# Sums of absolute weights moved to ScalarE, one norm spread over later units, one norm deferred, in a four-layer Perceiver kernel

## The reference, cut to what matters

```
x = x + L0_xattn(layernorm(x), ctx, ctx, mask)      # 16 heads over 4096 keys
x = x + L0_attn(...); x = x + L0_ffn(layernorm(x), w1, conv_w, conv_b, w2)
...                                                 # layer 1 and 2
x = x + L2_ffn(layernorm(x), W_r, W_k, W_v, mu_r, mu_k)   # sigmoid(r) * v
x = x + L3_xattn(layernorm(x), ctx, ctx, Wq, Wk, Wv, Wp, focusing_factor)
x = x + L3_attn(...); x = x + L3_ffn(...)
```

```
def weight_quant(w):
    scale = 1.0 / jnp.clip(jnp.mean(jnp.abs(w)), 1e-05)
    return jnp.clip(jnp.round(w * scale), -1, 1) / scale
```

## Time and profile before

| | us |
|---|---|
| three timed runs | 2000.08, 2008.40, 2007.03 |
| their median | 2007.03 |
| the profiled execution | 2001.91 |
| its span | 2000.6 |
| mean granted clock of PE in it | 0.989 |

### The profile page before, as it was taken

The page is one execution under the profiler, slowest core; times in us unless marked ns, Lnnn a source line. Parts: engine busy times, 40 slices in busy tenths (PEclk is TensorE's granted clock), DMA queues, the critical chain, the costliest instruction groups (busy, mean ns, idle before and its releaser), DMA issues.

```text
span 2000.6 us, 38492 instructions
## 1 busy us (share of the span) xinstructions
PE 1894.7 (95%) x14304; PEld 1204.0 (60%) x14329; DVE 1354.4 (68%) x3178; ACT 1248.9 (62%) x2811; POOL 706.3 (35%) x899
## 2 busy tenths in 40 slices
PE   7999999989999899999999999999999899899999
PEld 4555665545465645566555556879657688565656
DVE  3677668765486677766879577774356998578382
ACT  3687778867363458777888673367265786265251
POOL 2123331173460211333110155676042566355151
PEclk9999999987999999999999999999999999999999
DMA  9677668753011497766876113164102342200110
GB/s 214 145 147 150 120 120 164 127 92 106 1 43 53 77 149 148 152 118 122 164 128 93 37 52 98 49 204 123 48 22 77 93 120 61 90 1 9 43 57 11
DMA packets 114362, 191.58 MB, mean 96 GB/s; under 512 B 17224, under 2 KB 67201, under 8 KB 107649
## 3 DMA queue, kind: packets, MB, share of 16 engines
q1 hardware_dynamic: 113184, 188.11, 42.9%
q10 hardware_dynamic: 992, 1.02, 0.2%
HBM read 135.20 MB, written 2.69 MB: 69 GB/s over the span
## 4 chain that ended last, share of the span: by engine, by line
PE 66%; DVE 21%; ACT 7%; issue 2%; POOL 2%; DMA 1%; SPq 0%; POOLq 0%; ACTq 0%; DVEq 0%
DVE WK L900 10%; PE PS L837 8%; PE PS L708 8%; PE PS L738 6%; PE PS L381 5%; PE PS L389 4%; PE PS L696 4%; ACT WK L586 3%; PE PS L2499 2%; PE PS L539 2%; PE PS L2441 2%; PE PS L491 2%; PE PS L518 2%; PE PS L754 2%; PE PS L1369 1%
## 5 line engine op out<-in xcount | busy, mean ns | idle before, releaser
L900 DVE TENSOR_REDUCE WK<-PS 128x1 f32<-128x1024 f32 x512 | 621.1, 1223 | 218.4 <-PE PS L708 170.3
L1008 ACT ACTIVATE WK<-PS 128x512 f32<-128x512 f32 x840 | 464.9, 601 | 45.0 <-PE PS L708 30.8
L708 PEld LDWEIGHTS PS<-QSR,KSR 51*128 51x128 f32 x2048 | 253.3, 189 | 242.0 <-ACT WK L1008 92.0
L708 PE MATMUL PS<-QSR,KSR 51*128 51x256 f32 x2048 | 381.4, 309 | 8.9 <-DVE WK L900 0.9
L696 PE MATMUL PS<-KSR,QSR 51*128 51x512 f32 x1024 | 371.6, 452 | 3.6 <-DMA KSR<-scratch_mask 2.8
L837 PE MATMUL PS<-WK 128*32 128x256 f32 x2528 | 223.4, 400 | 0.5 <-ACT WK L992 0.5
L614 POOL TENSOR_SCALAR WK<-WK 128x256 f32<-128x256 f32 (+1 forms) x320 | 150.9, 472 | 164.3 <-ACT WK L586 62.9
L1023 POOL TENSOR_TENSOR WK<-WK 128x512 fp32r<-128x512 f32 x62 | 79.2, 1278 | 350.9 <-ACT WK L969 177.0
L696 PEld LDWEIGHTS PS<-KSR,QSR 51*128 51x128 f32 x1024 | 187.2, 187 | 13.2 <-DVE WK L900 6.5
L586 ACT ACTIVATE WK<-PS,WK 128x256 f32<-128x256 f32 (+1 forms) x320 | 140.4, 450 | 62.3 <-DVE WK L558 42.0
L1126 POOL TENSOR_SCALAR nbw<-WK 128x4 fp32r<-128x4 f32 x64 | 12.6, 197 | 314.2 <-DVE WK L906 313.3
(11 more groups left out here) (388 smaller groups left out, 3897.9 us busy)
## 6 DMA issues: line engine op xcount, KB each, us to landing
KSR<-WK SPq DMA_DIRECT2D x381, 128.0 KB
WB<-in_ctxT SPq DMA_DIRECT2D x78, 512.0 KB, 5.1
WK<-in_ctxT SPq DMA_DIRECT2D x40, 512.0 KB, 4.1
WK<-in_ctx SPq DMA_DIRECT2D x32, 512.0 KB, 3.9
WA<-in_ctxT SPq DMA_DIRECT2D x26, 512.0 KB, 5.1
QSR<-scratch_q SPq DMA_DIRECT2D x48, 128.0 KB, 4.4
WB<-in_L3f_qkv SPq DMA_DIRECT2D x2, 1536.0 KB, 6.3
WB<-in_L3f_w SPq DMA_DIRECT2D x2, 1536.0 KB, 10.2
```

Of the source, the lines that this page charges most:

```text
L708: return pe.e.matmul(tile["S", L, s, i][:, j * 256:j * 256 + 256], KS[s % 4][HALF[i % 2], kt * 128:(kt + 1) * 128], QS[HALF[i % 2], g % 2, ...
L900: dv.e.tensor_reduce(mt[:, n:n + 1], tile["R", L, s, n].rearrange("p a b -> p (a b)"), AX, ALU.max).then_inc(*dv.at("R", L, s, n))
L1008: ac.e.activation(PR[n % NPR], tile["S", L, s, i], ACT.Exp).then_inc(*ac.at("E", L, s, i))
```

## The change

Five edits:

- **A.** POOL's `magnitude` and `total` go. ACT instead takes |w| of 1024 columns with one instruction that also adds them up (`accum_out`), four times: behind the exponentials (26,5), (26,13), (27,5) and (27,9) of layer 0's cross attention. PE waits for the last of them at `M(28)` and adds two columns for each matrix, so four products stand where two stood.
- **B.** In layer 2's tail DVE only multiplies; the sum into X goes to POOL, one instruction for all four blocks, at the end of its u = 3. Mean and variance of the four blocks are taken by DVE at u = 4 to 7. ACT makes 1/sqrt by a logarithm and an exponential at u = 7, DVE the shift at u = 8, POOL the four normalised blocks at u = 8, PE the transposes at u = 9, with the banks of `ring3`.
- **C.** The queries are projected at u = 10, not 5. `again` becomes `{2: 7, 3: 9, 15: 9, 17: 9}`, and the transposes have no `filled`.
- **D.** `l2f` ends for DVE after the multiplications, so `l3x_sp` starts there.
- **E.** Of the four norms at `M(9)`, `M(17)`, `M(25)`, `M(33)` the first moves behind the row maximum `R(10,4)`, in both layers.

```diff
-        def turn_pe(tag, src, of, *by, filled=(0, 0, 0, 0)):
+        def turn_pe(tag, src, of, *by, filled=(0, 0, 0, 0), ring=None):
...
-                b = take(banks, (tag, f), (by[f], tag, f))
+                b = take(banks if ring is None else ring, (tag, f), (by[f], tag, f))
...
+        ABS = ((26, 5), (26, 13), (27, 5), (27, 9))
...
                     if L == 0 and s == 28:
+                        pe.wait_ge(ac, "wabs", 3)
                         for i in range(2):
-                            pe.wait_ge(po, "wabs", i)
                             pe.e.matmul(b.ap[:, 1, 384 + i:385 + i], onesf[:, :], wst[:, 4 * i:4 * i + 1], start=True,
+                                        stop=False)
+                            pe.e.matmul(b.ap[:, 1, 384 + i:385 + i], onesf[:, :], wst[:, 4 * i + 3:4 * i + 4], start=False,
                                         stop=True).then_inc(*pe.at("wsum", i))
...
+                    if s == 10 and n == 4:
+                        normalise(*late)
...
                     if s >= 2 and hh == 7:
...
+                        if s == 9:
+                            late = (g, bb)
                         else:
+                            normalise(g, bb)
...
                     ac.e.activation(PR[n % NPR], tile["S", L, s, i], ACT.Exp).then_inc(*ac.at("E", L, s, i))
+                    if L == 0 and (s, i) in ABS:
+                        j = ABS.index((s, i))
+                        ac.wait_ge(pe, "F", L, 23, 7)
+                        ac.wait_ge(d_l0f)
+                        ac.wait_ge(ac)
+                        ac.e.activation(WK[:, 16384:17408], WA[:, 1024 * j:1024 * j + 1024], ACT.Abs,
+                                        accum_out=wst[:, j // 2 * 4 + j % 2 * 3:j // 2 * 4 + j % 2 * 3 + 1]).then_inc(
+                            *ac.at("wabs", j))
...
-                    if L == 0 and s == 25:
-                        magnitude(0, 0)
-                        magnitude(0, 1)
-                    if L == 0 and s == 26:
-                        total(0)
-                        magnitude(1, 0)
-                    if L == 0 and s == 27:
-                        magnitude(1, 1)
-                        total(1)
...
                 dv.e.tensor_tensor(RR[:, t, :], tile["v2f", t][:, 0:256], RR[:, t, :], ALU.mult).then_inc(*dv.at("v2f", t))
-                dv.wait_ge(dv)
-                dv.e.tensor_tensor(X[:, t, :], X[:, t, :], RR[:, t, :], ALU.add).then_inc(*dv.at())
-                if t == NT - 1:
-                    end(dv, "l2f")
-                ln_a("ln3x", X, t)
-                if t:
-                    ln_b("ln3x", X, XN, t - 1)
-            ln_b("ln3x", X, XN, NT - 1)
+            end(dv, "l2f")
...
-        unit = [*range(1, 6), 0, *range(6, NU)]
+        unit = [*range(1, 11), 0, *range(11, NU)]
...
-            again = {2: 7, 3: 26, 10: 9, 17: 9}
+            again = {2: 7, 3: 9, 15: 9, 17: 9}
...
-                if u == 3:
-                    turn_pe("h3x", XN, (dv, "ln3x"), dv, ac, filled=(10, 4, 4, 0))
+                if u == 9:
+                    turn_pe("h3x", XN, (po, "ln3x"), dv, ac, ring=ring3)
...
-                if u == 3:
+                if u == 8:
+                    dv.wait_ge(ac, "ln3x", "rs")
+                    dv.e.scalar_tensor_tensor(out=wst[:, 16:20], in0=mv[:, :, 0], scalar=-1.0, in1=rs[:, :], op0=ALU.mult,
+                                              op1=ALU.mult).then_inc(*dv.at("ln3x", "mr"))
+                if u == 9:
                     turn_dve("h3x", 0)
                 if u < NU:
                     low3_dve(u)
+                if 4 <= u < 8:
+                    dv.wait_ge(po, "x2f")
+                    ln_a("ln3x", X, u - 4)
...
-                if u == 2:
-                    ln_act("ln3x")
-                    ac.e.preload_act_table_set("natural_log_exp_and_others")
-                if u == 3:
+                if u == 7:
+                    ac.wait_ge(dv, "ln3x", "var", NT - 1)
+                    ac.e.activation(rs[:, :], mv[:, :, 1], ACT.Ln, bias=epsl[:, 0:1], scale=1.0).then_inc(*ac.at())
+                    ac.wait_ge(ac)
+                    ac.e.activation(rs[:, :], rs[:, :], ACT.Exp, scale=-0.5).then_inc(*ac.at("ln3x", "rs"))
+                if u == 9:
                     turn_act("h3x", 1)
...
+                if u == 3:
+                    po.wait_ge(dv, "v2f", NT - 1)
+                    po.e.tensor_tensor(X[:, :, :], X[:, :, :], RR, ALU.add).then_inc(*po.at("x2f"))
+                if u == 8:
+                    po.wait_ge(dv, "ln3x", "mr")
+                    for t in range(NT):
+                        po.e.tensor_scalar(XN[:, t, :], X[:, t, :], rs[:, t:t + 1], wst[:, 16 + t:17 + t], ALU.mult,
+                                           ALU.add).then_inc(*po.at("ln3x", t))
```

More of the change, by code:

```diff
@@ L857, in xattn_dve, with normalise @@
         def xattn_dve(L):
+            def normalise(g, bb):
+                dv.wait_ge(dv)
+                dv.e.reciprocal(RC, OB[:, :, :, 16]).then_inc(*dv.at())
+                dv.wait_ge(dv)
+                rc = RC.rearrange("p q (h c) -> p q h c", c=1).to_broadcast([128, 2, 8, 16])
+                f = g % 2 * 128
+                o4 = (X, XN)[L][:, 2 * bb:2 * bb + 2, f:f + 128].rearrange("p q (h c) -> p q h c", c=16)
+                if L == 0:
+                    dv.e.tensor_tensor(OB[:, :, :, 0:16], OB[:, :, :, 0:16], rc, ALU.mult).then_inc(*dv.at())
+                    dv.wait_ge(dv)
+                    dv.wait_ge(po, "vb")
+                    dv.e.tensor_tensor(o4, OB[:, :, :, 0:16], o4, ALU.add).then_inc(*dv.at("norm", L, g))
+                else:
+                    dv.e.tensor_tensor(o4, OB[:, :, :, 0:16], rc, ALU.mult).then_inc(*dv.at("norm", L, g))
             if L:
@@ L935, in xattn_dve @@
                     if s >= 2 and hh == 7:
-                        dv.wait_ge(dv)
-                        dv.e.reciprocal(RC, OB[:, :, :, 16]).then_inc(*dv.at())
-                        dv.wait_ge(dv)
-                        rc = RC.rearrange("p q (h c) -> p q h c", c=1).to_broadcast([128, 2, 8, 16])
-                        f = g % 2 * 128
-                        o4 = (X, XN)[L][:, 2 * bb:2 * bb + 2, f:f + 128].rearrange("p q (h c) -> p q h c", c=16)
-                        if L == 0:
-                            dv.e.tensor_tensor(OB[:, :, :, 0:16], OB[:, :, :, 0:16], rc, ALU.mult).then_inc(*dv.at())
-                            dv.wait_ge(dv)
-                            dv.wait_ge(po, "vb")
-                            dv.e.tensor_tensor(o4, OB[:, :, :, 0:16], o4, ALU.add).then_inc(*dv.at("norm", L, g))
+                        if s == 9:
+                            late = (g, bb)
                         else:
-                            dv.e.tensor_tensor(o4, OB[:, :, :, 0:16], rc, ALU.mult).then_inc(*dv.at("norm", L, g))
+                            normalise(g, bb)
         def xattn_act(L, steps=None):
@@ L1059, in value_bias @@
                     po.e.tensor_tensor(X[:, t, :], X[:, t, :], vbt, ALU.add).then_inc(*po.at("vb"))
-            def size_of(i, j):
-                return WK[:, 16384 + 2048 * i + 1024 * j:17408 + 2048 * i + 1024 * j]
-            def magnitude(i, j):
-                w, size = WA[:, 2048 * i + 1024 * j:2048 * i + 1024 * j + 1024], size_of(i, j)
-                po.wait_ge(pe, "F", L, 23, 7)
-                po.wait_ge(d_l0f)
-                po.wait_ge(po)
-                po.e.tensor_scalar(size, w, 0.0, 2.0, ALU.max, ALU.mult).then_inc(*po.at())
-                po.wait_ge(po)
-                po.e.tensor_tensor(size, size, w, ALU.subtract).then_inc(*po.at())
-            def total(i):
-                half, a, b = 1024, size_of(i, 0), size_of(i, 1)
-                while half > 1:
-                    po.wait_ge(po)
-                    po.e.tensor_tensor(a[:, 0:half], a[:, 0:half], b[:, 0:half], ALU.add).then_inc(*po.at())
-                    half //= 2
-                    b = a[:, half:2 * half]
-                po.wait_ge(po)
-                po.e.tensor_tensor(wst[:, 4 * i:4 * i + 1], a[:, 0:1], a[:, 1:2], ALU.add).then_inc(*po.at("wabs", i))
             def quantise(i, j):
```

1 line of the change is left out of this document (removed).

## The result

The changed kernel takes 1983.9 us (median of 4 runs, 1981.58 to 1985.07); the kernel before took 2007.72 in the same comparison (4 runs, 2000.08 to 2009.35). The ratio is 0.9887, interval [0.986, 0.9914]: 1.1% faster. The interval is the 95% one of the ratio, so the gain is clear of the noise. The forecast was 1980.0 with a range of 1972 to 1993.

A forecast was written before the change was run, and what follows sets the result against it. PE (95% busy) was taken as the bound, except where POOL's sums stall it and halve its clock in layer 0's tail. 19.7 + 4.3 = 24.0 off 2001.91 gives 1977.9; with 2 us of runs' excess, 1980, range 1972 to 1993.

The forecast's parts named there:

- Edit A, 19.7 forecast: Layer 0's tail: removing POOL's sums gives back 23.7 us, ACT's Abs and the added products cost 4.0.
- the rival of the tables: Layer 0's tail: each Abs needs table loads on ACT, making the kernel slower than before, 2024 us; chance 0.04.
- the tail clock: Rival: the clock falls again in layer 0's tail, costing 6.9 and about 1.5 us, total 1988; chance 0.18.
- 10.2 idle and 13.5 of halved clock: Split of layer 0's tail excess over layer 1's, 23.74 us, into PE idle time and PE at half clock.
- The start of layer 3: Layer 3's cross attention: DVE's shorter layer 2 tail lets the first `gram` start earlier, gaining 9.7 to 10 us.
- The hole at u = 9: Layer 3's cross attention: PE waits for POOL's normalised blocks, giving back 5.4 us, bounds 0.9 and 7.
- a rival, at 2 to 8: Clock falls behind layer 3's hole at u = 9, losing 2 to 8 us; long fall 1988, chance 0.12.
- The norm's gain: Edits B and C in layer 3: 9.7 minus 5.4, 4.3 us gained, between -1 and 9.
- Edit D, also counted at nothing: Loads of `l3x_sp` come some 6.5 us earlier, before layer 3's attention; counted as no gain.
- 0, between -0.3 and 0.3: Deferred norm, step after `M(9)`: its 1.1 us lie in DVE's slack before and after, 0 for both layers.
- 2 us for the runs' excess over the profiled execution: Whole kernel: of the 5.1 us by which the runs' median exceeds the profiled execution, 2 are kept.

The follow-up runs named there:

- the run with the short Abs: Changed kernel without edit E, each of the four Abs reading one column of the weights instead of 1024: 1979.3 us, ratio 0.9879.
- The runs with filled waits: Kernel before plus unread products ahead of PE's waits for `nb` in layer 0's tail: steps 26, 28, 2003.34 us; steps 26, 27, 28, 2000.12 us.

## Why the prediction was right

- **Edit A, 19.7 forecast.** The tail lost 20.6. The Abs and the added products cost 3.2 over layer 1's 78.27 instead of 4.0: an Abs took 1.06 + 0.18, overlapping, where I took 1.3, and PE waited 0.41 on average, not 0.9. Those four waits are 1.65 in all, but the run with the short Abs puts 2.5 on the sums' length, and 0.65 on the rest, where I had 3.6 and 0.4. No table was loaded, so the rival of the tables is out; the granted clock was 1.00 from 400 to 484, so the tail clock is out too. The Trainium skill states (ScalarE: Activation LUTs, section "Table sets: the hidden batching unit") that abs is in every table set; the trace, with no load among the four, agrees. Right, and shown by the run with A alone.
- **"10.2 idle and 13.5 of halved clock"** was a wrong reading with a right sum. The runs with filled waits give 15.3 to POOL's chain up to `M(28)` (47.9 - 32.6) and 8.4 to the clock behind. It did no harm because edit A takes both. Had the change only filled the waits, I would have forecast 13.5 in the tail, and it was 7.3.
- **The start of layer 3, 9.7 forecast:** the first `gram` came 9.6 earlier, 10.36 us behind the first multiplication for 19.92.
- **The hole at u = 9, 5.4 forecast.** From the transposes before it (1592.23) to `v3k` (1596.71) 4.5 us, 4.7 forecast. But behind it came 1.7 of half clock (1.58 for 1.07, 4.88 for 3.68), which I had only as a rival, at 2 to 8. There was another 1.7 of half clock behind the gap at u = 4, not in my sum. The norm's gain became 1.9 in this profile instead of 4.3: of the 9.6, 7.7 were given back and not 5.4. The kernel before had no fall there. Without any, the gain is 144.82 - 141.25 = 3.6; the fall at u = 9 took 1.6 more, that at u = 4 was hidden by ACT. Timed alone, B to D give 0.9985 [0.9962, 1.0009], not to be told from nothing. Edit D, also counted at nothing, has no run of its own.
- **Edit E, "0, between -0.3 and 0.3": failed, by -1.8 us.** "DVE busy 11.17 of 15.60" is an average over a step; at the place of the norm, PE wants the next reduction at once for its PSUM pair. The price of the norm's work was wrong too: its multiplication stands beside POOL's 128x512 instruction and takes 0.4 and 0.6 us more, which by the rows above is 1.0 of the 1.8. Nor did I see what the edit avoids: a chance meeting of the same kind that costs 0.7 or 5.6 us in layer 0 in six of the nine profiles without it, and 0.3 or 0.4 in layer 1 in two.
- **2 us for the runs' excess over the profiled execution** was about right: the changed kernel's median lies 2.3 above its own profiled execution. That was a guess between 0 and 5, and of four runs against three, so partly luck.

The errors add: +0.9 for A, -2.4 for the norm, -1.8 for E, together -3.3 from 24.0, which gives the spans' 20.7. It comes out so evenly because the differences outside the change (+2.35, -1.9, -0.4) happen to cancel. The main term, edit A, is right by its mechanism; the norm's term and E's were too good by 4.2 together, of which the excess in A hides 0.9. The ratios of the parts timed alone multiply to the whole: 0.9918 x 0.9985 x 0.9990 = 0.9893, where the changed kernel has 0.9887.

## What to carry to other kernels

Split a stall's damage into idle time and half clock only after asking who sets the pace at half clock: while another engine's chain is late anyway, the slower PE costs nothing, as with POOL's 41.1 us here at either clock. An engine's mean slack in a step says nothing about a given place in it; look at which buffer the next consumer wants and whose release stands behind the inserted work. When two-operand DVE work on SBUF stands beside POOL work on SBUF by chance, profile several times, or move it where they can't meet; and look at what it meets in the new place, which I did not for edit E.
